# Attention scores of both attention layers as three rounded products, with keys and queries split on three engines

## What is computed

```python
# layer 0: 16 query heads, 4 key/value heads, head size 96; keys = 361 context tokens + 100 latents
q = (latents @ Wq.T).reshape(b, q_len, H, HD)
k = (hidden @ Wk.T).reshape(b, s_len, KV, HD)
scores = jnp.einsum('bkgqd,bksd->bkgqs', q, k) * scale
attn = jax.nn.softmax(scores, axis=-1)
out = jnp.einsum('bkgqs,bksd->bkgqd', attn, v)
x = x + tanh(g) * (out.reshape(b, q_len, H * HD) @ Wo.T)
# layer 1: 32 query heads, 8 key/value heads, head size 128; keys = 361 context tokens;
# q and k pass an rmsnorm per head first
```

## Time and profile before

| | before |
|---|---|
| median of three runs | 2783.17 us (2781.26 to 2789.91) |
| profiled execution, its time | 2777.63 us |
| its span in the profile | 2775.8 us |
| TensorE matmul busy | 2517.4 us, 91% |
| VectorE busy | 1455.6 us, 52% |
| ScalarE busy | 827.3 us, 30% |
| GpSimd busy | 533.8 us, 19% |
| DMA moved | 217.40 MB, mean 78 GB/s |

### The profile page before, as it was taken

The page is one execution under the profiler, slowest core; times in us unless marked ns, Lnnn a source line. Parts: engine busy times, 40 slices in busy tenths (PEclk is TensorE's granted clock), DMA queues, the critical chain, the costliest instruction groups (busy, mean ns, idle before and its releaser), DMA issues. The chain is left out here.

```text
span 2775.8 us, 32483 instructions
## 1 busy us (share of the span) xinstructions
PE 2517.4 (91%) x12384; PEld 2109.7 (76%) x12384; DVE 1455.6 (52%) x2473; ACT 827.3 (30%) x1922; POOL 533.8 (19%) x414
## 2 busy tenths in 40 slices
PE   8999999799996899998769689999999999998824
PEld 6888888589995677776569468888888888886723
DVE  6222222223102576667543546666666766766697
ACT  3222222223212333333210234333333333332323
POOL 3000000000002122211021143334334334331120
PEclk9999999899997999999989889999999999999766
DMA  6222222253222222222021113323323223322001
GB/s 197 69 69 69 69 69 62 74 173 105 68 90 85 62 79 88 80 70 61 12 69 39 55 58 95 103 84 102 101 85 103 95 90 103 93 78 75 9 0 48
DMA packets 159357, 217.40 MB, mean 78 GB/s; under 512 B 31511, under 2 KB 124083, under 8 KB 158179
## 3 DMA queue, kind: packets, MB, share of 16 engines
q1 hardware_dynamic: 159202, 215.33, 25.4%
HBM read 176.99 MB, written 38.29 MB: 78 GB/s over the span
## 5 line engine op out<-in xcount | busy, mean ns | idle before, releaser
L1034 POOL TENSOR_TENSOR attend_w_hi<-attend_w_raw,attend_one 128x1024 fp32r<-128x1024 f32 (+1 forms) x184 | 335.9, 1840 | 478.6 <-DMA attend_w_raw<-in_wo 284.6
L1326 PE MATMUL attend_ps_score<-attend_k_in,attend_q 128*100 128x361 f32 (+1 forms) x768 | 298.1, 512 | 18.6 <-ACT attend_p L1078 11.0
L1271 PE MATMUL attend_ps_gemm<-normed_hi,attend_w_hi 128*128 128x400 f32 x704 | 268.3, 381 | 39.0 <-DVE attend_w_lo L1156 39.0
L1271 PE MATMUL attend_ps_gemm<-attend_o_hi,attend_w_hi 128*128 128x400 f32 x704 | 274.0, 389 | 27.0 <-DVE attend_w_lo L1156 24.5
L1156 DVE TENSOR_TENSOR attend_w_lo<-attend_w_raw,attend_w_hi 128x1024 fp32r<-128x1024 f32 (+1 forms) x184 | 216.7, 1212 | 155.8 <-POOL attend_w_hi L1034 154.8
L1081 ACT ACTIVATE attend_p<-attend_p,attend_neg_max 100x361 f32<-100x361 f32 x256 | 150.8, 590 | 398.0 <-DVE attend_neg_max L1181 398.0
L1271 PE MATMUL attend_ps_gemm<-attend_o_hi,attend_w_lo 128*128 128x400 f32 x704 | 244.7, 348 | 0.0
L1271 PE MATMUL attend_ps_gemm<-normed_lo,attend_w_hi 128*128 128x400 f32 x704 | 244.4, 347 | 0.0
L1271 PE MATMUL attend_ps_gemm<-attend_o_lo,attend_w_hi 128*128 128x400 f32 x704 | 244.2, 347 | 0.0
L1271 PE MATMUL attend_ps_gemm<-normed_hi,attend_w_lo 128*128 128x400 f32 x704 | 243.5, 346 | 0.0
L1211 DVE SCALAR_TENSOR_TENSOR stream_tokens<-attend_ps_gemm,attend_gate,stream_tokens 128x400 f32<-128x400 f32 x192 | 121.4, 633 | 230.3 <-PE attend_ps_gemm L1271 229.7
(11 more groups left out here) (252 smaller groups left out, 5071.4 us busy)
## 6 DMA issues: line engine op xcount, KB each, us to landing
attend_w_raw<-in_wq SPq DMA_DIRECT2D x88, 512.0 KB, 3.8
attend_w_raw<-in_wo SPq DMA_DIRECT2D x64, 512.0 KB, 5.1
attend_w_raw<-in_wo SPq DMA_DIRECT2D x32, 384.0 KB, 3.5
context_ctx_raw<-in_ctxT SPq DMA_DIRECT2D x8, 1456.0 KB
attend_k_in<-scratch_k SPq DMA_DIRECT2D x64, 180.5 KB
context_ctx_raw<-in_ctxF SPq DMA_DIRECT2D x22, 512.0 KB
scratch_v<-context_v_out SPq DMA_DIRECT2D x44, 256.0 KB, 2.2
scratch_k<-context_kt_out SPq DMA_DIRECT2D x44, 256.0 KB, 5.0
```

The source lines that it names most:

```text
L1034: pool.tensor_tensor(hi, w_flat(w_raw, j % RAW, j), one[:hi.shape[0]].to_broadcast(hi.shape), ALU.mult).then_inc(w_hi_done, 1)
L1271: mm = pe.matmul(out, left[a](c), right[b](c), start=(c == 0 and a == b == 0), stop=(c == chunks - 1 and a == 1))
L1326: pe.matmul(ps_score[:S, h % 2, :NK], q[:, i % 2, h, k * S:(k + 1) * S], k_in[:, u % KV_SLOTS], start=True, stop=True).then_inc(s_done, 1)
```

## The change

Scores become three rounded products, like the projections. In `attend`:

- The ring `k_in` becomes three of two slots: `k_raw` (loaded), `k_hi` and `k_lo`. One column is added (`NKE` = 362 or 462 in place of 361 or 461), and set to zero once.
- GpSimd makes `k_hi` by a multiplication with one and `k_lo` by a subtraction (`split_keys`), three units ahead, ahead of its weights in each step.
- ScalarE's copy of the query now writes the rounded type (`q_hi`); VectorE takes the remainder from PSUM (`remainder_q`), at the end of its step. The PSUM bank of a query projection comes free when that remainder is taken, not when ScalarE has copied.
- A score head is three matmuls (q_hi k_hi, q_hi k_lo, q_lo k_hi) in place of one f32 matmul.
- Rings shrink: `RAW` 3 to 2 in layer 1 (3 in layer 0), `SPLIT` 4 to 3, values from 4 slots to 3, the split squares from two buffers to one.
- On SyncE's queue keys and values have waits of their own: a key slot is loaded again when its split is done, a value slot when the product with values is done.

```diff
-    RAW, SPLIT = 3, 4
-    P_SLOTS, KV_SLOTS = 3, 4
-    KV_DMAS = 3
+    RAW, SPLIT = 3 - layer, 3
+    P_SLOTS, K_SLOTS, V_SLOTS = 3, 2, 3
+    V_DMAS = 2
...
+            def keys(u):
...
+                if u >= K_SLOTS:
+                    sp.wait_ge(k_lo_done, u - K_SLOTS + 1)
...
+                sp.dma_start(k_raw[:, slot, 0:NK], src).then_inc(k_load[slot], 16)
...
             for u in range(NU):
-                kv(u + KV_SLOTS - 1)
+                keys(u + K_SLOTS + 1)
+                values(u + V_SLOTS - 1)
                 for j in step_tiles(u + 2):
                     tile(j)
...
+            def split_keys(u):
...
+                pool.wait_ge(k_load[slot], (u // K_SLOTS + 1) * 16)
+                if u >= K_SLOTS:
+                    pool.wait_ge(s_done, (u - K_SLOTS + 1) * HG)
+                pool.tensor_tensor(k_hi[:, slot], k_raw[:, slot], one[:HD].to_broadcast([HD, NKE]), ALU.mult
+                                   ).then_inc(k_hi_done, 1)
+                pool.wait_ge(k_hi_done, u + 1)
+                pool.tensor_tensor(k_lo[:, slot], k_raw[:, slot], k_hi[:, slot].bitcast(F32), ALU.subtract
+                                   ).then_inc(k_lo_done, 1)
...
             for u in range(NU):
+                split_keys(u + 3)
                 for j in step_tiles(u + 1):
                     weights(j)
                 squares(query_of(u))
...
-                act.activation(q[:, i % 2, h], ps_gemm[:HD, bank, :HT], ACT.Copy).then_inc(q_read, 1)
+                act.activation(q_hi[:, i % 2, h], ps_gemm[:HD, bank, :HT], ACT.Copy).then_inc(q_read, 1)
...
+            def remainder_q(n):
...
+                dve.wait_ge(q_read, (n + 1) * Q_COPIES)
+                dve.tensor_tensor(q_lo[:, i % 2, h], ps_gemm[:HD, bank, :HT], q_hi[:, i % 2, h].bitcast(F32), ALU.subtract
+                                  ).then_inc(q_lo_done, 1)
...
                 for j in step_tiles(u + 1):
                     split(j)
+                remainder_q(query_of(u))
...
-                        pe.wait_ge(q_read, (at + 1) * Q_COPIES)
+                        pe.wait_ge(q_lo_done, (at + 1) * Q_COPIES)
...
-                    pe.matmul(ps_score[:S, h % 2, :NK], q[:, i % 2, h, k * S:(k + 1) * S], k_in[:, u % KV_SLOTS],
-                              start=True, stop=True).then_inc(s_done, 1)
+                    at = slice(k * S, (k + 1) * S)
+                    for a, b in ((q_hi, k_hi), (q_hi, k_lo), (q_lo, k_hi)):
+                        mm = pe.matmul(ps_score[:S, h % 2, :NKE], a[:, i % 2, h, at], b[:, u % K_SLOTS],
+                                       start=(a is q_hi and b is k_hi), stop=(a is q_lo))
+                    mm.then_inc(s_done, 1)
```

More of the change, by code:

```diff
@@ L876, in attend @@
         ps_sum = ps("ps_sum", [P, BANK])
-        w_load = [sem("w_load0"), sem("w_load1"), sem("w_load2")]
+        w_load = [sem(f"w_load{slot}") for slot in range(RAW)]
         w_hi_done = sem("w_hi_done")
         w_lo_done = sem("w_lo_done")
-        kv_load = [sem("kv_load0"), sem("kv_load1"), sem("kv_load2"), sem("kv_load3")]
+        k_load = [sem("k_load0"), sem("k_load1")]
+        v_load = [sem("v_load0"), sem("v_load1"), sem("v_load2")]
+        k_hi_done = sem("k_hi_done")
+        k_lo_done = sem("k_lo_done")
         gemm_done = sem("gemm_done")
         q_read = sem("q_read")
+        q_lo_done = sem("q_lo_done")
         o_read = sem("o_read")
@@ L995, in _ @@
                 tile(j)
-            for u in range(KV_SLOTS - 1):
-                kv(u)
+            for u in range(K_SLOTS):
+                keys(u)
+            for u in range(V_SLOTS - 1):
+                values(u)
             for j in range(RAW, LEAD):
@@ L1001, in _ @@
                 tile(j)
+            keys(K_SLOTS)
             for u in range(NU):
-                kv(u + KV_SLOTS - 1)
+                keys(u + K_SLOTS + 1)
+                values(u + V_SLOTS - 1)
                 for j in step_tiles(u + 2):
                     tile(j)
-        CONSTS = 10 if layer == 1 else 3
+        CONSTS = 11 if layer == 1 else 4
         @block.gpsimd
@@ L1157, in split @@
                                   w_flat(w_hi, j % SPLIT, j).bitcast(F32), ALU.subtract).then_inc(w_lo_done, 1)
+            def remainder_q(n):
+                if n is None:
+                    return
+                i, h = n // QT, n % QT
+                bank = gemm_at["q", n, 0] % 2
+                dve.wait_ge(q_read, (n + 1) * Q_COPIES)
+                dve.tensor_tensor(q_lo[:, i % 2, h], ps_gemm[:HD, bank, :HT], q_hi[:, i % 2, h].bitcast(F32), ALU.subtract
+                                  ).then_inc(q_lo_done, 1)
+                if layer == 0:
+                    last = slice(h * REST, (h + 1) * REST)
+                    dve.tensor_tensor(q_lo[last, i % 2, HG - 1], ps_gemm[HD:P, bank, :HT],
+                                      q_hi[last, i % 2, HG - 1].bitcast(F32), ALU.subtract).then_inc(q_lo_done, 1)
             def maxima(u, pair):
@@ L1212, in accumulate @@
                                          tokens[:, m, at], ALU.mult, ALU.add).then_inc(o_read, 1)
-            for j in range(LEAD):
+            for j in range(SPLIT):
                 split(j)
+            for j in range(SPLIT, LEAD):
+                remainder_q(j - SPLIT)
+                split(j)
+            for n in range(LEAD - SPLIT, LEAD):
+                remainder_q(n)
             if layer == 1:
@@ L1303, in sum_squares @@
                     pe.wait_ge(r_rooted, i)
[L1304 to L1305 removed]
+                pe.matmul(ps_sum[:HG, :HT], head_pick[:, h], square_hi[:], start=(h == 0), stop=False)
+                pe.matmul(ps_sum[:HG, :HT], head_pick[:, h], square_lo[:], start=False,
                           stop=(h == HG - 1)).then_inc(q_summed, 1)
```

57 lines of the change are left out of this document (35 added, 22 removed).

## The result

The change made the kernel slower: 2832.45 us (median of 4 runs, 2827.39 to 2835.03) against 2783.76 us before (median of 4 runs), ratio 1.0169, 95% interval [1.0148, 1.0191]. The prediction was 2746 us. The profiled execution took 2832.57 us.

A forecast was written before the change was run, and what follows sets the result against it. TensorE, busy 91% of the span, was taken as the bound; savings of 23.2 + 9.8 + 3.0 + 0.9 = 37 us, all else 0, took the median from 2783.2 to 2746 us, range 2729 to 2768.

The forecast's parts named there:

- TensorE's term: Score heads as three rounded matmuls, 0.166 us each at 362 columns, 0.207 at 462; 37 us saved in all.
- Rivals 3 and 4: No change at 2783 us if a rounded score costs 0.2 us (chance 0.04); 2729 us if columns alone set distance (0.05).
- GpSimd and the rings: Layer 1's weight loop takes 12.3 us against TensorE's 14.4 us step, leaving 2.1 us of room: cost 0.
- rival 1: Layer 1's weight loop becomes the bound if GpSimd's operations take long values: 17.0 us a step, 2889 us, chance 0.06.
- In steady steps the key split falls 5 to 7 us into the step, when VectorE is waiting for sums: Argument that GpSimd's key split would not run beside busy VectorE in full steps, so long values would not occur.
- One buffer for the squares: One split-squares buffer in place of two: emptied 4 us into a step, before the next split, so cost 0.
- VectorE's remainder of the query: New subtraction out of PSUM at VectorE's step end, 0.57 us, taken up by 0.66 and 2.36 us idle: cost 0.
- Starts: Beginning of each layer: later first maximum and shorter score pairs about even; 0, bounds -1 and +2 us.
- The gain of layer 0: Shorter scores in layer 0: 9.8 us in 16 steps with a query projection, 3.0 us in 10 steps without.

The follow-up runs named there:

- keys_once: The changed kernel, but GpSimd splits only the keys of each layer's first two units, which all later units read; 2761.0 us, ratio 0.993.
- early_gate: The changed kernel with the keys' load one iteration earlier and GpSimd's key split waiting for VectorE's weight splits of the step; 2782.4 us, ratio 1.001.
- fold_early_gate: The changed kernel with early_gate's placing in both layers and layer 0's bias factor put on the query; 2761.9 us, ratio 0.9939.
- tt_normalise: The changed kernel with normalising and layer 0's bias scaling given two tensor inputs instead of one and a scalar; 2884.7 us, ratio 1.0372.
- raw3: The changed kernel with three weight slots instead of two and two value slots instead of three in layer 1; 2802.2 us, ratio 1.0078.
- dummy_beside: The kernel before, plus two unread GpSimd operations per layer 1 unit, held until the second pair of scores is done; 2817.0 us, ratio 1.0133.

## Why the prediction was wrong, point by point

- **TensorE's term: right in price.** 362 columns: (2238.01 - 2237.34) / 4 = 0.1675 us from start to start against the 0.166 taken; over the whole layer the median distance is 0.165, and for 462 columns 0.211 against 0.207. Where the rest was out of the way (keys_once, early_gate, fold_early_gate) a step of layer 1 is 14.4 us and the layer 23.2 to 23.4 us shorter, where 24 were summed. Rivals 3 and 4 fell.
- **GpSimd and the rings, "The loop has 2.1 us of room: cost 0": this step failed.** Its first three terms held: from the end of the last remainder to the keys it was 5.86 us (5.6 taken), the key split took 1.81 (1.7), the two roundings 3.95 (3.76). The last term was one remainder, 1.2 us, as if VectorE stood ready. It was 4.38 us, from 2251.19 to 2255.57: VectorE was still in the held normalising, the output's remainder came next, and the remainders of the weights themselves were held by the split of the squares (3.46 us for two, 2.35 before). That makes 16.0 us in this step in place of 12.3, over the 14.4 of TensorE. For layer 0 the prediction has no such sum: it prices GpSimd's work there at 2.2 us a unit and then puts it at nothing. There the operation on the maxima took 1049 ns in place of 278 and the normalising 552 in place of 464, and the layer lost 30.6 us of the 55.
- **The contention was weighed on the wrong instructions.** The prediction looked at the two that the trace had shown long, rounding and remainder of weights, and asked in rival 1 whether *they* would stretch. It did not ask which other VectorE instructions are of the kind that collides. In the trace after, the normalising, the operation on the maxima ("the bias") and the weights' remainder wait for GpSimd; the maximum over SBUF does not (0.91 us in the row above), nor does what reads PSUM (mask and scale, 582 ns on average in the changed kernel, 593 before). Not one of the 384 normalising and 64 bias instructions lies inside the span of a GpSimd instruction; 57 of the 96 reciprocals and 64 of the 256 of mask and scale do. The Trainium skill ("GPSIMD Engine Reference", section 1) names VectorE instructions "in a 2-port perf mode or with two SBUF inputs"; which mode an instruction ran in no run here shows, but the tensor-scalar rows (423 to 897 ns) fit the first kind, the rows of tt_normalise the second, and the maximum, 0.91 us beside GpSimd, neither. The rule was in the prediction, and was applied to one of three operations.
- **"In steady steps the key split falls 5 to 7 us into the step, when VectorE is waiting for sums": too short a look.** The roundings come behind the key split, and by the prediction's own terms they end 5.6 + 1.7 + 3.76 = 11.1 us after the last remainder. In the step of the earlier trace rows of the kernel before that remainder ended at 2217.45 and normalising started at 2227.82, so the second rounding would have run to 2228.5, beside it:

```profile
2216.23 1.22 DVE L1156 TENSOR_TENSOR attend_w_lo<-attend_w_raw,attend_w_hi 128x1024 fp32r<-128x1024 f32 x1
...
2227.82 1.36 DVE L1192 TENSOR_SCALAR attend_p<-attend_p,attend_exp_inv 100x361 f32<-100x361 f32 x4
```

  Once it is held, the next remainders end later, and with them the loads: in the step shown above the key split starts 9.1 us in (2245.43 after 2236.35).
- **Rival 1 was the right neighbour.** Its place, the weight loop of two slots, decided in layer 1, as raw3 shows. Its price of 17.0 us per step was near the 16.0 of this one by luck: it had GpSimd's operations at their long values (2.6 and 5.9 us), and they took 1.81 and 3.95; the long term was VectorE's. And full steps lie between 14.5 and 16.8 us, 15.0 on average, so that the layer lost 11 us to before instead of 119. It said nothing of layer 0, which lost most, 30.6 us.
- **One buffer for the squares, cost 0: right, though TensorE now waits for them.** keys_once has one buffer and waits for the split 3 times in layer 1, as before; dummy_beside has two and waits 43 times. It is the hold, not the buffer.
- **VectorE's remainder of the query, cost 0: right.** keys_once has it in both layers and its steps are 14.4 us.
- **"Starts", 0 with bounds -1 and +2 us: missed in layer 0.** Its first values come at 910.91 us against 906.06, 4.9 us later. In keys_once they come at 906.06, so this goes with the key split too. The stretch from layer 0's last values to layer 1's first is unchanged (319.7 us against 319.9).
- **The gain of layer 0, 12.8 us: not there, even undisturbed.** keys_once has 14.4 and 11.9 us for the two kinds of step, as forecast, and yet only 1.6 us less in all. The windows of some of its steps beside the same steps of the kernel before (us from:to, length, busy TensorE, granted clock):

```profile
920.00:936.50 16.50, 14.61 (x62) 0.81 0.17 46
...
965.00:978.50 13.50, 12.27 (x56) 0.87 0.32 96
...
1317.00:1330.50 13.50, 10.92 (x44) 0.75 0.10 30
```

```profile
919.10:933.30 14.20, 12.76 (x57) 0.94 0.19 53
...
961.80:974.00 12.20, 11.23 (x51) 1.00 0.35 99
...
1321.40:1332.10 10.70, 7.86 (x44) 1.00 0.12 38
```

  Where TensorE waits for other engines, part of what a shorter score product saves goes into a longer wait (1.24 us in place of 0.96 in the steps without query projection). The granted clock was 1.00 (2.4 GHz) in every step of keys_once in which TensorE never waits, and below it in seven of the fifteen in which it does; before, in three of fifteen: 0.87 where it had been 1.00, 0.75 where it had been 1.00. Over the layer it is 0.96 against 0.99. The sum took the clock as given. These rows fit a saving that was paid back there, some 11 us, a second term that was mis-sized; no run held the clock to show it.
- **The end of the program** took 215.2 us in the one profile of the kernel before and 219.9 to 224.4 in all others, the two with f32 scores in both layers among them (219.9 and 220.3). It is not shown that the change does this; the clock there was 0.69 before, 0.65 after.

The losses add up in the profiled executions: +30.6 in layer 0, +11.0 in layer 1, +8.7 at the end and +4.9 before the first values of layer 0, together the 55 us of 2830.8 - 2775.8.

## What to carry to other kernels

Before work goes to GpSimd, list VectorE's instructions whose operands are all in SBUF and see, from the loop that feeds GpSimd, at what point of the step its work will stand: beside VectorE's work on PSUM it was free, beside its tensor-scalar and two-tensor work on SBUF one engine waited until the other's instruction had ended. A maximum and a reciprocal on SBUF were free here, so look for each kind of instruction in a trace. An idle engine's room in a step is worth nothing without its place, and the place is set by the last wait ahead of it, here a load behind a ring of two slots. And check the last term of a loop too: an engine that closes it must be free then, not only on average.

## What the runs showed of the hardware that was not expected

A tensor-scalar instruction of VectorE on SBUF does not share with GpSimd but waits: two elements per row took 3.47 us in place of 0.17, through three GpSimd instructions on end, so the wait is not set by its size. In layer 0 the smallest operation lost most, 49 us of busy time against 11 for the normalising. It goes both ways: the split of a square on GpSimd, 0.85 us, took 1.87 us on average in the changed kernel, beside VectorE's remainder of weights. Moving an operation to two tensor inputs made it slower (520 ns against 392 at the least for 361 columns) and did not free it.
